# A Mamba layer between two feed-forward layers: the out projection as products of rounded halves

## Chip, cores and metric

One core of a Trainium2 chip. The metric is the device time of one execution in microseconds. Before the change three runs gave 1508.79, 1508.95 and 1509.53 us (median 1508.95).

## What is computed

The input is one sequence of 2048 tokens with 256 channels, float32. Three residual steps follow each other, each behind a layer norm: a gated feed-forward layer whose weights are looked up in a table of 16 values, a Mamba-2 layer of 64 heads of 64 channels with a state of 128, and the feed-forward layer again.

```python
x = x + 0.5 * ffn(layernorm(x))
x = x + mamba2(layernorm(x))
x = x + 0.5 * ffn(layernorm(x))
```

What matters of the Mamba layer (the reference works in chunks of 32 tokens, the kernel in chunks of 128, which gives the same sums):

```python
gate, hbc, dt = split(h @ in_proj_w)
hbc = silu(causal_conv4(hbc) + conv_b)              # x, B, C
dt = softplus(dt + dt_bias); cum = cumsum(-exp(A_log) * dt)
Y_diag = (C B^T * exp(cum_i - cum_j) * dt) @ x      # within a chunk
Y_off = exp(cum) * (C @ prev_states)                # from the chunks before
hidden = (Y_diag + Y_off + D * x) * silu(gate)
hidden = hidden * rsqrt(mean(hidden ** 2) + EPS) * norm_w
out = hidden @ out_proj_w
```

## The kernel before

The program is written out instruction by instruction: each engine (TensorE, VectorE, ScalarE, GpSimd, and SP, which issues the loads and stores) has a block with its own sequence, and semaphores order the engines among each other. An engine carries out its sequence strictly in the order in which it is written, so an instruction that waits holds up everything behind it.

First the weights of the feed-forward layer are decoded and that layer runs (24 ticks); the small projections for B, C and dt are made in its last ticks. Then comes the loop over the Mamba layer, from about 345 to 1368 us, and a second block with the second feed-forward layer.

The loop has 128 slots. The 64 heads are 32 pairs, taken in 8 groups of 4 pairs (GP = 4); a group goes through the 4 tiles of 512 tokens (TT), and in each tile through its 4 pairs. Slot v is thus pair v % 4 of its group and tile v // 4 % 4; 16 slots make a group. The loop is software-pipelined. In its step s (loops in lines 637, 903, 1009, 1311, 1616):

- TensorE (PE): states(s+2), turn_x(s+3) (a transpose), diag(s+1), the gate and x projections proj_g and proj_x of s+8, out_proj(s), off(s+2). The two projections are made of rounded halves (float32r): split_matmul gives hi x hi, hi x lo and lo x hi. The out projection is two exact fp32 products, on wo and hid.
- VectorE (DVE): the three conv taps of s+7 between the scans of s+2 (which carry the state from chunk to chunk), times_dt(s+3), skip_path(s+1) (writes hid), masked(s+2), scale_off(s+2), and after every fourth slot add_out(s), which takes the sum of four pairs out of PSUM.
- ScalarE (ACT): square(s), relus and exps of s+3 (the decays), evac_g and evac_x of s+8. With s % 4 = 0, here called the silu slot, the silus of four pairs come together between two loads of the activation table.
- GpSimd (POOL): add_squares(s), to_chunk_end(s+3) (makes xend, which the states need), in the silu slot the halo sums for the conv (not for tile 0), and gate(s+1), which multiplies hid by silu of the gate.
- SP: loads of cum_row(s+5), which waits for relus, and behind it e_row(s+4), and the weights of the next group.

The weights of the next group are prepared within a group by slot number u = s % 16: ScalarE makes the high halves (split_g_hi in u 6 and 8, split_x_hi in u 6 to 9) and scales the out weights (scale_wo in u 13 to 15 and in u 0 of the next group); GpSimd makes the low halves. They come at the end of the step of their engine.

## Time and profile before

| | |
|---|---|
| median of three runs | 1508.95 us |
| profiled execution, its time | 1511.01 us |
| profiled execution, its span | 1509.2 us |
| instructions in the span | 26250 |
| mean granted TensorE clock | 0.967 of full speed |

The profile is of one execution. Its page gives the busy time of each engine, and groups of instructions by line; the timeline gives instructions in order of time, with "idle before" in square brackets and the instruction that ended the idle time behind the arrow. "x4" counts instructions that were merged to one row; an exact fp32 product shows as two. The end of a matmul is modelled, so differences of starts say more than the lengths in the rows. PE is TensorE, PEld its weight loads.

### The profile page before, as it was taken

The page shows a single profiled execution, that of the slowest core. Times are in us where ns is not written, and L with a number is a line of the kernel's source. Part 1 is how long each engine was busy: PE and PEld are TensorE (multiplying, and loading weights), DVE is VectorE, ACT ScalarE, POOL GpSimd, SP SyncE. Part 2 cuts the span into 40 slices and gives each one's busy share as a digit, 9 for nine tenths or more (in the row PEclk, how much of TensorE's full clock was granted, in tenths as well). Part 3 has the DMA queues.
Part 4 walks back from the last instruction along what each step waited for, and adds up shares of the span by engine and source line. Part 5 has one row for each costly group of instructions (what it writes and reads, how often), then busy time and mean ns, then how long its engine had stood idle before and what let it go on. Part 6 is the DMA issues. An engine that isn't in the chain of part 4 may idle for free. (4 is left out here: it accounts for less than half of the span.)

```text
span 1509.2 us, 26250 instructions
## 1 busy us (share of the span) xinstructions
PE 1388.3 (92%) x8704; PEld 1091.1 (72%) x8704; DVE 1128.3 (75%) x2547; ACT 1040.4 (69%) x2133; POOL 680.6 (45%) x637
## 2 busy tenths in 40 slices
PE   4889977768999999999999999999999999986998
PEld 4878766556777777777777777777777777764787
DVE  5752444666988888897888889788888979896433
ACT  0124333576988888898888889888888988871332
POOL 1013211023656666566666656666665665661000
PEclk9999989889999999999999999999999999996999
DMA  5220000224344444343453533445444434334000
GB/s 125 71 88 25 15 15 14 69 43 102 106 105 113 123 104 114 99 107 105 110 127 100 112 98 113 103 113 122 108 108 93 116 103 112 101 95 181 15 14 28
DMA packets 102079, 136.36 MB, mean 90 GB/s; under 512 B 27744, under 2 KB 49856, under 8 KB 101824
## 3 DMA queue, kind: packets, MB, share of 16 engines
q1 hardware_dynamic: 99840, 132.67, 33.8%
q10 hardware_dynamic: 2112, 2.10, 0.4%
q8 instruction: 68, 1.11, 0.3%
q14 instruction: 59, 0.48, 0.1%
HBM read 124.76 MB, written 9.96 MB: 89 GB/s over the span
## 5 line engine op out<-in xcount | busy, mean ns | idle before, releaser
L843 ACT ACTIVATE M<-cum_row,cum_table 128x128 f32<-128x128 f32 x1024 | 311.8, 389 | 0.0
L1204 DVE SCALAR_TENSOR_TENSOR xs<-psum,conv_w_sb,xs 128x509 f32<-128x509 f32 (+2 forms) x384 | 284.9, 742 | 0.4
L994 POOL TENSOR_TENSOR xend<-xdt,to_end_table 128x512 f32<-128x512 f32 x128 | 148.9, 1164 | 298.1 <-DVE xdt L1215 298.1
L1592 PE MATMUL psum<-hid,wo 128*128 128x512 f32 x512 | 242.8, 596 | 9.1 <-ACT eT L754 8.8
L1000 POOL TENSOR_TENSOR hid<-hid,sg 128x512 f32<-128x512 f32 x128 | 241.8, 1889 | 0.1
L986 POOL TENSOR_TENSOR squares<-squares,sq 128x512 f32<-128x512 f32 x124 | 158.7, 1280 | 118.9 <-ACT sq L820 118.3
L1252 DVE TENSOR_TENSOR psum<-psum,e_row 128x512 f32<-128x512 f32 x128 | 89.5, 699 | 122.3 <-PE psum L1566 117.9
L1225 DVE TENSOR_TENSOR M<-M,CB 128x1024 f32<-128x1024 f32 x128 | 177.7, 1388 | 0.0
L1592 PEld LDWEIGHTS psum<-hid,wo 128*128 128x128 f32 x512 | 96.2, 189 | 84.1 <-issue 72.3
L1552 PE MATMUL psum<-xend,B_tok 128*128 128x128 f32 x1024 | 139.0, 279 | 17.5 <-POOL xend L994 17.2
L1577 PE MATMUL psum<-M,xdt 128*64 128x128 f32 x2048 | 142.7, 282 | 1.0 <-DVE psum L1252 0.9
L1552 PEld LDWEIGHTS psum<-xend,B_tok 128*128 128x128 f32 x1024 | 126.2, 194 | 22.7 <-POOL xend L994 21.7
L857 ACT ACTIVATE xs<-psum,conv_b_sb,conv_w_sb 128x512 f32<-128x512 f32 x128 | 98.6, 770 | 52.8 <-PE psum L40 47.2
L851 ACT ACTIVATE M<-M 128x1024 f32<-128x1024 f32 x128 | 134.4, 1050 | 0.5
L1577 PEld LDWEIGHTS psum<-M,xdt 128*64 128x64 f32 x2048 | 111.4, 138 | 22.9 <-issue 22.9
L825 ACT ACTIVATE sg<-psum 128x512 f32<-128x512 f32 x128 | 74.8, 585 | 75.7 <-PE psum L40 67.5
L1245 DVE SCALAR_TENSOR_TENSOR inner<-inner,decay_table,psum 128x64 f32<-128x64 f32 x512 | 118.3, 273 | 0.0
L38 PE MATMUL psum<-xT_hi,gw_hi 128*128 128x512 f32 x256 | 115.3, 450 | 2.2 <-DVE x_res L1062 1.5
L946 POOL TENSOR_TENSOR ffn_hidden_lo<-ffn_hidden,ffn_hidden_hi 128x512 fp32r<-128x512 f32 x24 | 30.8, 1284 | 182.6 <-ACT ffn_hidden_hi L669 182.6
L820 ACT ACTIVATE sq<-hid 128x512 f32<-128x512 f32 x124 | 77.6, 626 | 48.4 <-POOL hid L1000 48.2
L1566 PE MATMUL psum<-CT,inner 128*128 128x128 f32 x768 | 106.7, 275 | 0.0
L40 PE MATMUL psum<-xT_hi,gw_lo 128*128 128x512 f32 x256 | 102.2, 399 | 0.0
(200 smaller groups left out, 3024.3 us busy)
## 6 DMA issues: line engine op xcount, KB each, us to landing
cum_row<-cum_scratch SPq DMA_DIRECT2D x256, 256.0 KB, 4.4
e_row<-e_scratch SPq DMA_DIRECT2D x256, 128.0 KB, 3.5
xw_raw<-L_attn_in_proj_w_dram SPq DMA_DIRECT2D x32, 128.0 KB, 3.0
wo_raw<-L_attn_out_proj_w_dram SPq DMA_DIRECT2D x32, 128.0 KB, 3.1
gw_raw<-L_attn_in_proj_w_dram SPq DMA_DIRECT2D x16, 256.0 KB, 6.5
x_res<-_attn_hidden_states_dram ACTq DMA_DIRECT2D x4, 512.0 KB, 9.9
x_scratch<-x_res SPq DMA_DIRECT2D x4, 512.0 KB, 2.6
x_res<-x_scratch SPq DMA_DIRECT2D x1, 2048.0 KB, 8.7
```

The costliest lines, as they stand in the source:

```text
L38: nc.tensor.matmul(out, l_hi, r_hi, start=start, stop=False, skip_group_check=skip)
L843: last = nc.scalar.activation(M[:, v % 3, h, c * CH:(c + 1) * CH], cum_row[:, v % 2, h, c * CH:(c + 1) * CH], ACT.Relu, bias=scalar_of(CUM ...
L851: nc.scalar.activation(M[:, v % 3], M[:, v % 3], ACT.Exp, scale=-1.0).then_inc(exp_done, 1)
L986: nc.gpsimd.tensor_tensor(squares[:, tile(t)], squares[:, tile(t)], sq[:], ALU.add).then_inc(squares_done, 1)
L994: nc.gpsimd.tensor_tensor(xend[:, v % 2], xdt[:, v % 3], per_chunk_head(TO_END, v), ALU.mult).then_inc(xend_done, 1)
L1000: nc.gpsimd.tensor_tensor(hid[:, v % 2, :], hid[:, v % 2, :], sg[:, v % 8, :], ALU.mult).then_inc(hid_done, 1)
L1204: nc.vector.scalar_tensor_tensor(xs[:, v % 8, shift:], psum[:, X_BANK + v % 2, 0:TT - shift], tap_of(v, step), xs[:, v % 8, shift:], ALU.m ...
L1225: nc.vector.tensor_tensor(M[:, v % 3], M[:, v % 3], cb, ALU.mult).then_inc(M_done, 1)
L1245: nc.vector.scalar_tensor_tensor(after, before, scalar_of(CHUNK_DECAY, v, chunk, h), psum[:, ST_BANK, c * P + h * HP:c * P + (h + 1) * HP] ...
L1552: last = nc.tensor.matmul(psum[:, ST_BANK, c * P:(c + 1) * P], B_tok[:, t * CPT + c, :], xend[:, v % 2, c].rearrange("p h q -> p (h q)"), ...
L1577: last = nc.tensor.matmul(psum[h * HP:(h + 1) * HP, Y_BANK, c * CH:(c + 1) * CH], xdt[:, v % 3, c, h, :], M[:, v % 3, h, c * CH:(c + 1) * CH],
L1592: last = nc.tensor.matmul(psum[:, OUT_BANK + m, :], wo[:, j, m * P:(m + 1) * P], hid[:, v % 2, :], start=(j == 0), stop=(j == GP - 1))
```

## The change

The out projection is made of rounded halves, as the other projections are: six products (three for each half of the 256 output channels) instead of two.

- VectorE copies hid to hid_hi (hid_to_hi, rounded, two buffers) after the first scan of the step. GpSimd subtracts to make hid_lo (one buffer) at the start of its step. out_proj waits for both; skip_path waits for hid_lo_done instead of out_done.
- The weights: ScalarE scales wo_raw in place and copies to wo_hi; GpSimd makes wo_lo (split_wo_lo). The last of a group moves from u 0 to u 1.
- ScalarE's square(s+1) moves into the silu slot, between relus and exps.
- To make room, gw_raw is halved (each half of the gate weights is loaded when the one before is split; the splits move from u 6 and 8 to u 6 and 9), e_row and xend have one buffer instead of two and xdt two instead of three. e_row is loaded one slot later.
- The zero state is left out: in tile 0 the first chunk has no off product, its scan is a copy, and the scaling leaves its columns out.
- In the front the splits and scalings are put on ticks 4 to 7, 12 and 15.

The core of the diff:

```diff
-    gw_raw = sb("gw_raw", [P, KT, GP * P], F32)
+    gw_raw = sb("gw_raw", [P, KT, GP * P // 2], F32)
...
-    wo = sb("wo", [P, GP, D], F32)
...
+    wo_hi = sb("wo_hi", [P, GP, D], F32R)
+    wo_lo = sb("wo_lo", [P, GP, D], F32R)
...
-    e_row = sb("e_row", [P, 2, TT], F32)
-    xdt = sb("xdt", [P, 3, CPT, 2, HP], F32)
-    xend = sb("xend", [P, 2, CPT, 2, HP], F32)
+    e_row = sb("e_row", [P, TT], F32)
+    xdt = sb("xdt", [P, 2, CPT, 2, HP], F32)
+    xend = sb("xend", [P, CPT, 2, HP], F32)
     inner = sb("inner", [P, 2, CPT - 1, 2, HP], F32)
     carry = sb("carry", [P, 2, GP, 2, HP], F32)
+    hid_hi = sb("hid_hi", [P, 2, TT], F32R)
     hid = sb("hid", [P, 2, TT], F32)
+    hid_lo = sb("hid_lo", [P, TT], F32R)
...
+    G_TICKS = (4, 7)
+    WO_TICKS = (5, 6, 12, 15)
...
             def load_g_weights(q):
 
                 half = GP * P // 2
-                if q >= 2:
-                    sp.wait_ge(gw_lo_done, q - 1)
-                else:
-                    sp.wait_ge(w_small_lo, 2)
-                at = q % 2 * half
-                sp.dma_start(gw_raw[:, :, at:at + half], w_in_t[:, :, q * half:(q + 1) * half]).then_inc(gw_in[q % 2], 16)
+                if q >= 1:
+                    sp.wait_ge(gw_lo_done, q)
+                sp.dma_start(gw_raw[:], w_in_t[:, :, q * half:(q + 1) * half]).then_inc(gw_in, 16)
 
             def load_wo(p):
                 if p >= 2:
-                    sp.wait_ge(wo_done, p - 1)
+                    sp.wait_ge(wo_lo_done, p - 1)
...
-                sp.wait_ge(off_scaled, nth(v - 2))
+                sp.wait_ge(off_scaled, nth(v - 1))
...
-                if alive(s + 4):
-                    load_e(s + 4)
+                if alive(s + 3):
+                    load_e(s + 3)
                 g, u = divmod(s, SLOTS)
                 if s < 0 or g == GROUPS - 1:
                     continue
@@ -646,13 +650,14 @@
                     load_x_weights((g + 1) * GP + u - 2)
                 if u == 4:
                     load_g_weights(2 * (g + 1))
+                if u == 7:
...
             def scale_wo(p):
                 act.wait_ge(wo_in[p % 2], (p // 2 + 1) * 16)
                 if p < GP:
                     act.wait_ge(chan_in, 80)
-                else:
+                    act.wait_ge(w_small_lo, 2)
+                nc.scalar.activation(wo_raw[:, p % 2, :], wo_raw[:, p % 2, :], ACT.Copy,
+                                     scale=norm_sb[:, p:p + 1]).then_inc(wo_done, 1)
+                if p >= GP:
                     act.wait_ge(out_done, nth(last_of(p - GP)))
-                nc.scalar.activation(wo[:, p % GP, :], wo_raw[:, p % 2, :], ACT.Copy,
-                                     scale=norm_sb[:, p:p + 1]).then_inc(wo_done, 1)
+                act.wait_ge(wo_done, p + 1)
+                nc.scalar.activation(wo_hi[:, p % GP, :], wo_raw[:, p % 2, :], ACT.Copy).then_inc(wo_hi_done, 1)
...
-                if alive(s):
+                if alive(s) and (s < 0 or s % GP != 1):
...
+                if s >= 0 and s % GP == 0:
+                    square(s + 1)
...
-                if g < GROUPS - 1 and u in (6, 8):
-                    split_g_hi(2 * (g + 1) + u // 2 - 3)
+                if g < GROUPS - 1 and u in (6, 9):
+                    split_g_hi(2 * (g + 1) + u // 3 - 2)
                 if g < GROUPS - 1 and 6 <= u < 6 + GP:
                     split_x_hi((g + 1) * GP + u - 6)
                 if g < GROUPS - 1 and u >= 13:
                     scale_wo((g + 1) * GP + u - 13)
-                if g > 0 and u == 0:
+                if g > 0 and u == 1:
...
+            def split_wo_lo(p):
+                pool.wait_ge(wo_hi_done, p + 1)
+                if p >= GP:
+                    pool.wait_ge(out_done, nth(last_of(p - GP)))
+                nc.gpsimd.tensor_tensor(wo_lo[:, p % GP, :], wo_raw[:, p % 2, :], wo_hi[:, p % GP, :].bitcast(F32),
+                                        ALU.subtract).then_inc(wo_lo_done, 1)
+
+            def hid_to_lo(v):
+                pool.wait_ge(hid_hi_done, nth(v))
+                pool.wait_ge(out_done, nth(v - 1))
+                nc.gpsimd.tensor_tensor(hid_lo[:], hid[:, v % 2, :], hid_hi[:, v % 2, :].bitcast(F32),
+                                        ALU.subtract).then_inc(hid_lo_done, 1)
...
+                    hid_to_lo(s)
...
+                if g > 0 and u == 1:
+                    split_wo_lo(g * GP + GP - 1)
                 if s < 0 or g == GROUPS - 1:
                     continue
-                if u in (6, 8):
-                    split_g_lo(2 * (g + 1) + u // 2 - 3)
+                if u in (6, 9):
+                    split_g_lo(2 * (g + 1) + u // 3 - 2)
                 if 6 <= u < 6 + GP:
                     split_x_lo((g + 1) * GP + u - 6)
+                if u >= 13:
+                    split_wo_lo((g + 1) * GP + u - 13)
...
+            def hid_to_hi(v):
+                dve.wait_ge(hid_done, nth(v))
+                dve.wait_ge(out_done, nth(v - 2))
+                nc.vector.tensor_copy(hid_hi[:, v % 2, :], hid[:, v % 2, :]).then_inc(hid_hi_done, 1)
...
+                if chunk == 0:
+                    nc.vector.tensor_copy(inner[:, v % 2, 0].rearrange("p h q -> p (h q)"),
+                                          psum[:, ST_BANK, 0:P]).then_inc(scan_step, 1)
+                    return
...
-                nc.vector.tensor_tensor(bank(Y_BANK), bank(Y_BANK), e_row[:, v % 2, :], ALU.mult).then_inc(off_scaled, 1)
+                dve.wait_ge(e_in, (v + 1) * 32)
+                cols = slice(CH if at_slot(v)[1] == 0 else 0, TT)
+                nc.vector.tensor_tensor(psum[:, Y_BANK, cols], psum[:, Y_BANK, cols], e_row[:, cols],
+                                        ALU.mult).then_inc(off_scaled, 1)
 
             def skip_path(v):
                 j, t = at_slot(v)
                 dve.wait_ge(diag_done, nth(v))
-                dve.wait_ge(out_done, nth(v - 2))
...
+                if alive(s):
+                    hid_to_hi(s)
...
-                for c in range(CPT):
-                    if c > 0:
-                        before = inner[:, v % 2, c - 1]
-                    else:
-                        before = zero_state[:] if t == 0 else carry[:, t % 2, j]
+                first = 1 if t == 0 else 0
+                for c in range(first, CPT):
...
-                pe.wait_ge(hid_done, nth(v))
-                pe.wait_ge(wo_done, pair_of(v) + 1)
+                pe.wait_ge(hid_hi_done, nth(v))
+                pe.wait_ge(hid_lo_done, nth(v))
+                pe.wait_ge(wo_lo_done, pair_of(v) + 1)
...
-                    last = nc.tensor.matmul(psum[:, OUT_BANK + m, :], wo[:, j, m * P:(m + 1) * P], hid[:, v % 2, :],
-                                            start=(j == 0), stop=(j == GP - 1))
+                    cols = slice(m * P, (m + 1) * P)
+                    last = split_matmul(nc, psum[:, OUT_BANK + m, :], wo_hi[:, j, cols], wo_lo[:, j, cols],
+                                        hid_hi[:, v % 2, :], hid_lo[:], start=(j == 0), stop=(j == GP - 1))
```

## Rows read from the trace of the kernel before

**Rows 1.** The page: busy time of each engine over the span.

```profile
PE 1388.3 (92%) x8704; PEld 1091.1 (72%) x8704; DVE 1128.3 (75%) x2547; ACT 1040.4 (69%) x2133; POOL 680.6 (45%) x637
```

**Rows 2.** Timeline, TensorE, one plain slot: start us, length us, engine, line, operation.

```profile
763.41 0.40 PE L38 MATMUL psum<-xT_hi,xw_hi 128*128 128x512 f32 x1
...
764.81 1.88 PE L1592 MATMUL psum<-hid,wo 128*128 128x512 f32 x4
...
766.52 0.38 PE L1566 MATMUL psum<-CT,carry 128*128 128x128 f32 x2
...
767.41 1.06 PE L1552 MATMUL psum<-xend,B_tok 128*128 128x128 f32 x8
```

**Rows 3.** Timeline, VectorE, a plain slot from one scaling on.

```profile
791.65 0.70 DVE L1252 TENSOR_TENSOR psum<-psum,e_row 128x512 f32<-128x512 f32 x1 [1.20 <-PE psum L1566]
...
797.15 1.25 DVE L1225 TENSOR_TENSOR M<-M,CB 128x1024 f32<-128x1024 f32 x1
```

**Rows 4.** Groups by line and shape, before 345 us: total us, mean ns.

```profile
L1121 DVE TENSOR_TENSOR zmax<-zmax,ez 128x512 f32<-128x512 f32 x2 | 1.4, 691 | 0.1
...
L1118 DVE TENSOR_SCALAR ez<-ez 128x512 f32<-128x512 f32 x2 | 0.8, 414 | 0.0
...
L946 POOL TENSOR_TENSOR ffn_hidden_lo<-ffn_hidden,ffn_hidden_hi 128x512 fp32r<-128x512 f32 x24 | 30.8, 1284 | 182.6 <-ACT ffn_hidden_hi L669 182.6
```

**Rows 5.** Timeline, VectorE, adding out, then the silu slot.

```profile
768.22 1.28 DVE L1273 TENSOR_TENSOR mixed<-psum,mixed 128x512 f32<-128x512 f32 x2
...
774.37 1.25 DVE L1225 TENSOR_TENSOR M<-M,CB 128x1024 f32<-128x1024 f32 x1
...
777.00 0.22 DVE L1200 SCALAR_TENSOR_TENSOR xs<-psum,conv_w_sb,halo_sum 128x3 f32<-128x3 f32 x1 [0.54 <-POOL halo_sum L977]
```

**Rows 6.** Timeline, ScalarE, the same silu slot and the next.

```profile
777.35 1.28 ACT L851 ACT_TABLE_LOAD   x1
...
782.95 0.76 ACT L857 ACTIVATE xs<-psum,conv_b_sb,conv_w_sb 128x512 f32<-128x512 f32 x1
```

**Rows 7.** Timeline, GpSimd, a plain slot: the gate beside the masked product.

```profile
797.31 2.23 POOL L1000 TENSOR_TENSOR hid<-hid,sg 128x512 f32<-128x512 f32 x1
```

**Rows 8.** Timeline, TensorE: the output projections of four slots that follow each other.

```profile
796.79 1.88 PE L1592 MATMUL psum<-hid,wo 128*128 128x512 f32 x4
...
804.74 1.88 PE L1592 MATMUL psum<-hid,wo 128*128 128x512 f32 x4
...
812.83 1.88 PE L1592 MATMUL psum<-hid,wo 128*128 128x512 f32 x4
...
822.91 1.88 PE L1592 MATMUL psum<-hid,wo 128*128 128x512 f32 x4
```

**Rows 9.** Timeline, GpSimd and then TensorE, about slots 8 and 9.

```profile
812.24 1.29 POOL L958 TENSOR_TENSOR gw_lo<-gw_raw,gw_hi 128x512 fp32r<-128x512 f32 x1 [3.56 <-ACT gw_hi L693]
...
818.62 0.73 POOL L952 TENSOR_TENSOR xw_lo<-xw_raw,xw_hi 128x256 fp32r<-128x256 f32 x1
...
817.48 1.16 PE L1552 MATMUL psum<-xend,B_tok 128*128 128x128 f32 x8 [1.88 <-POOL xend L994]
```

**Rows 10.** Timeline, TensorE: diagonal products in slot 10 of two groups.

```profile
686.78 1.98 PE L1577 MATMUL psum<-M,xdt 128*64 128x128 f32 x16
...
819.00 1.09 PE L1577 MATMUL psum<-M,xdt 128*64 128x128 f32 x16
```

**Rows 11.** Timeline, GpSimd, two gates among the last slots.

```profile
1344.77 2.25 POOL L1000 TENSOR_TENSOR hid<-hid,sg 128x512 f32<-128x512 f32 x1
...
1350.00 2.26 POOL L1000 TENSOR_TENSOR hid<-hid,sg 128x512 f32<-128x512 f32 x1
```

**Rows 12.** Timeline, TensorE, states of slot 2 of a group.

```profile
882.19 1.16 PE L1552 MATMUL psum<-xend,B_tok 128*128 128x128 f32 x8 [0.36 <-POOL xend L994]
```

**Rows 13.** Groups by line in 340 to 1400 us: scans from the zero state.

```profile
L1245 DVE SCALAR_TENSOR_TENSOR inner<-zero_state,decay_table,psum 128x64 f32<-128x64 f32 x58 | 13.4, 274 | 0.0
```

**Rows 14.** The page: DMA issues; KB of each, us from issue to landing.

```profile
e_row<-e_scratch SPq DMA_DIRECT2D x256, 128.0 KB, 3.5
```

78 lines of the change are left out of this document (40 added, 38 removed).

## Prediction

> **What bounds the kernel now.** I began with the page's busy times. TensorE is busy for 92% of the span, VectorE for 75%, ScalarE for 69% and GpSimd for 45% [rows 1]. In the loop that the change edits, which holds most of the span, an average of the whole span hides how close the engines are, so I read one slot (one pair of heads times one tile of 512 tokens) on the timeline, engine by engine.
>
> TensorE: the six products of the x projection begin at 763.41, the output projection at 764.81, the off-diagonal products at 766.52, and the states of the next slot at 767.41 [rows 2]. So six rounded (split) products take 1.40 us, the two exact fp32 products of the output projection take 1.71 (the row's 1.88 is a modelled end; I use starts), and four off products take 0.89. From one output projection to the next are 7.95 us (796.79 to 804.74) and TensorE has no gap in them [rows 8]. A plain slot is bound by TensorE.
>
> VectorE in a plain slot: it waits 1.20 us for the off products before scaling them, and nowhere else [rows 3]. So it has 6.75 us of work. But once in four slots it also adds out the projection (1.28 us, start to next start 1.20), after which it is late: in that next slot (the silu slot, first of four) TensorE has to wait for VectorE's skip path before its off products, and the slot after begins with a 0.54 us wait for the halo sums [rows 5]. Four slots take 31.98 us (764.81 to 796.79 [rows 2, 8]) against 4 x 7.945 = 31.78.
>
> GpSimd has one more limit. Its gate takes 1.28 us of its own (as the same form of operation does elsewhere [rows 4]) but 2.23 when it starts beside the 1.25 us masked product of VectorE [rows 3, 7]. These two exclude one another.
>
> The worst slot: from 812.83 to 822.91 are 10.08 us [rows 8]. GpSimd waited 3.56 us for gw_hi, which ScalarE makes only at the end of the silu slot, so xend came late and TensorE waited 1.88 [rows 9]. That is 2.1 us in each of seven groups of sixteen slots. In three of the seven TensorE's granted clock then fell to the lower level (1.2 GHz) for some 3 us: the diagonal products, 1.09 at the upper level, took 1.98 [rows 10], and with the other products of those 3 us the slot was 1.55 longer again (from the starts of its output projections).
>
> **The change, part by part.** Durations are of the profiled execution; I add the sum to the median.
>
> 1. *Output projection, TensorE.* Six rounded products for two exact ones: 1.71 becomes 1.40, less 0.31 us in a slot. If TensorE bound all 128 slots, 40 us would go. With the plain slot then at 7.95 - 0.33 = 7.62 (0.02 by the closer spacing of such products, an estimate from [rows 2]).
>
> 2. *High half, VectorE.* Not in the trace. The nearest rows: a one-source operation over 128x512 from SBUF to SBUF took 414 ns, a two-source one 691 [rows 4]. I take 0.41 (start to start about 0.35, as all VectorE operations here follow some 0.07 before the modelled end), since a copy has one source; 0.69 stays as the upper bound, and the lower is 0.35, as the copy is certainly not free. It stands after the first scan, so everything of VectorE's queue waits for it, and it waits for the gate of the same head pair.
>
> VectorE then needs 6.75 + 0.35 = 7.10 in a plain slot, plus about 0.15 between the masked product and the scaling, which was hidden in the wait: 7.3. That is below 7.62. In the silu slot it starts 2.02 behind TensorE (0.82 as in a plain slot and 1.20 for adding out). Skip path done 5.5 after its start means off products at 7.55 rather than 6.73: the silu slot takes 8.5. In the next slot VectorE is 0.8 behind and waits 0.55 for halo sums (masked product to halo sum is unchanged, 2.63 us from 774.37 to 777.00 [rows 5]): 7.8. Then two of 7.62. Sum 31.6 against 31.98: **-0.4 us for four slots**, and not -1.3.
>
> 3. *Low half, GpSimd.* 1.28 us by the same form [rows 4]. It waits for hid_hi, and behind it in GpSimd's queue stand the squares, xend and the next gate. In a plain slot it ends 3.0 us after VectorE's slot began, 1.3 before the output projection wants it, and xend still follows its own input. So it is hidden where GpSimd has no other work. Where GpSimd also splits weights, it is not: with a split of gate weights (1.3) and x weights (0.7 [rows 9]) behind the gate, xend lands on the masked product and delays it by 0.4 to 0.8.
>
> By the Trainium skill, "SBUF — State Buffer", section "SBUF: two separate sides", VectorE and GpSimd lock a shared pair of ports for a whole instruction, for two SBUF inputs or a two-port mode; the gate's 2.23 agrees. By "VectorE: DVE Perf Modes", section "The perf-mode tier table", an fp32 copy within SBUF runs at two elements a cycle, which fits 414 ns and would make the copy a holder of that lock as well.
>
> 4. *Square moved ahead in the silu slot.* ScalarE ends its relus, then waits for the gate of the next slot, squares, and only then loads the exp table (at 777.35 now, right behind the relus [rows 6]). That wait is about 0.6 us, and with the square (0.53) the exps and all behind them come 1.1 later: evac_x, started at 782.95 now, reaches VectorE's next slot 0.3 late, which still fits into slack. In exchange GpSimd gets the square about 2 us sooner. The 0.36 wait of TensorE for xend at the third slot of a group [rows 12] goes, with 0.2 of slower starts around it: -0.6 for a group.
>
> 5. *Gate-weight split from slot 8 to slot 9, one raw buffer.* In slot 8 the x split remains, and GpSimd still waits for ScalarE's end of the silu slot before it; behind it now stand the x split (0.7), the masked product (1.25), the low half (1.28), squares (1.3) and xend (1.05). I get xend 5.5 us after GpSimd's restart, where today 5.2 pass (812.24 to 817.48 [rows 9]); and the output projection itself now waits, because the low half comes after that same point. Output projection of slot 8 to the states of slot 10 was 12.7; I get about 13.9: **+1.2 in each of seven groups**. The stall of TensorE is then over 3 us, so I take the lower clock in all seven instead of three: 4 x 1.55 = **+6.2**.
>
> 6. *Zero state left out* (tile 0, four of sixteen slots): one of four off chunks, 0.22, and a pair of scans of 274 ns [rows 13] replaced by a copy of 0.2 to 0.3: about -0.35 for a pair of slots.
>
> 7. *e_row with one buffer.* The load waits for the same scaling as before, but is needed one slot sooner. It lands 3.5 us after issue [rows 14] and has over 6: hidden, by 1 us in the silu slot, where it is queued on SP behind cum_row. xdt and xend with one buffer fewer wait for products that are over by then: nothing. Norm scaling of wo becomes scale and copy, one pass more on ScalarE, and 0.7 on GpSimd (the shape of the x split [rows 9]), four times in a group; in slots 1 and 13 to 15 this costs 0.5, as a late xend pushing the masked product. In the front the same steps, +1 us at most.
>
> 8. *The end.* The last slots have no projections; GpSimd binds them already, a gate every 5.23 us [rows 11]. Low half in that chain: +1.1 for some five slots, and +1.5 before the last product: **+6**.
>
> **Sum.** A group: slots 0 to 3: -0.4 - 0.6 - 0.35 + 0.5 = -0.85. Slots 4 to 7: -0.4 + 0.2 (splits) = -0.2. Slots 8 to 11: -0.4 + 1.2 + 0.1 = +0.9. Slots 12 to 15: -0.4 - 0.4 (the last tile has a pair of scans fewer, so the copy fits) - 0.3 (tile 0) + 0.1 = -1.0. Together -1.15, for seven groups -8; the last group -1; clock +6; end +6; front +1. That is +4. The profiled execution's span was 1509.2 and its time 1511.0, the median of the runs 1508.95; so I forecast 1508.95 + 4 to 5, **1514**.
>
> **Rivals.** *The gain survives (faster).* If VectorE's lateness is absorbed, the silu slot and the next stay at 7.95 and the others get 7.62: 31.14 for four, -0.84 x 32 = -27; tile 0 adds -7, the end +5: 1480. For it: TensorE has no gap in plain slots. Against: VectorE's slot with adding out is already 8 us of work. *The copy runs at one element a cycle (slower):* 0.69 instead of 0.41 is 0.28 more in the three slots of four where VectorE decides: 0.75 x 32 = +24: 1538. It decides from a copy of about 0.45. For it only that the output is of the rounded type; against it the 414 ns row. *More collisions of masked product and GpSimd (slower):* GpSimd's four operations, the copy and the masked product exclude each other and fill 6.6 of 7.9 us; if each four slots lose 0.5 more, 1530. *The change does not do what it says:* six products with six weight loads could run slower than the projections' 1.40, but those have the same shapes; I give it nothing.
>
> **How the numbers follow.** Forecast case 0.50, of which I give 0.06 to faster by over 0.2%, 0.12 to within and 0.32 to slower, as its terms are each good to some tenths of a us in 16 slots. The gain survives 0.30 (0.27 faster, 0.03 same). Slow copy 0.10 and more collisions 0.10, both slower. So faster 0.33, same 0.15, slower 0.52; 0.2% (3 us) is about what a measurement of this kernel can tell from no change. The forecast case alone spans 1500 to 1528. The range reaches halfway into the surviving gain, to 1482, and to the slow copy, 1540.
>
> **What would show it.** Right: output projection 1.40 start to start; hid_hi at 0.41; plain slots 7.6, silu slots 8.5; a stall of over 3 us at the output projection of slot 9 in each group, with the lower clock behind it; last slots over 6 us. Wrong: silu slots at 8 or less, slot 9 no longer than 10 us, hid_hi near 0.7, or masked products mostly over 1.6. A loss in a wait for e_row or for gw_raw would be a mechanism that I count at nothing.

## The result, and the profile after

The changed kernel takes 1526.32 us (median of 4 runs, 1518.78 to 1526.84) against 1509.01 for the kernel before in the same session: ratio 1.0103, 95% interval 1.0076 to 1.0130. It is slower by 17 us where I had forecast 5. The profiled execution is the quickest of the four (span 1517.1, mean granted clock 0.969); the other three had spans of 1524.5 to 1525.1 at clocks of 0.961 to 0.964.

The first lines of the page of after, in the columns of [rows 1]:

```profile
PE 1346.9 (89%) x8896; PEld 1127.2 (74%) x8896; DVE 1168.8 (77%) x2643; ACT 1050.9 (69%) x2165; POOL 868.0 (57%) x796
```

TensorE is busy for less time, as the change wants, and the span is longer. GpSimd has gone from 45% to 57%.

TensorE, timeline of after (start, us, instruction, count, idle time before it and what ended it). First the slot with the stall, then the output projection and what follows it in the next; the last row is of slot 14, which step 7 below comes back to:

```profile
812.65 0.47 PE L38 MATMUL psum<-hid_hi,wo_hi 128*128 128x512 f32 x1 [3.58 <-issue]
...
813.48 0.63 PE L38 MATMUL psum<-hid_hi,wo_hi 128*128 128x512 f32 x1
...
814.76 0.63 PE L1605 MATMUL psum<-CT,carry 128*128 128x128 f32 x2
815.18 1.49 PE L1605 MATMUL psum<-CT,inner 128*128 128x128 f32 x6
816.47 1.19 PE L1593 MATMUL psum<-xend,B_tok 128*128 128x128 f32 x8
...
821.94 0.39 PE L38 MATMUL psum<-hid_hi,wo_hi 128*128 128x512 f32 x1
822.17 0.40 PE L39 MATMUL psum<-hid_lo,wo_hi 128*128 128x512 f32 x1
...
823.32 0.38 PE L1605 MATMUL psum<-CT,carry 128*128 128x128 f32 x2
...
856.56 1.16 PE L1593 MATMUL psum<-xend,B_tok 128*128 128x128 f32 x8 [1.01 <-POOL xend L1016]
```

The output projection takes 1.38 us (821.94 to 823.32), and from it to the next are 7.61 (the next starts at 829.55). From the same rows over the whole loop come the distances between output projections, which I compare in four parts of a group of sixteen slots (slot 0 is the silu slot of tile 0). One group of each kernel from the same part of the loop (slot 9 is 10.08 in four groups before and about 11.65 in three; after, it is 9.2 to 9.3 in five and 7.68 in two), slots 0 to 3, 4 to 7, 8 to 11, 12 to 15:

| | 0-3 | 4-7 | 8-11 | 12-15 |
|---|---|---|---|---|
| before | 8.15 8.57 7.95 7.95 | 8.15 7.95 7.94 7.95 | 8.09 **10.08** 7.95 7.95 | 7.95 8.26 7.95 7.95 |
| after | 7.94 8.00 7.91 7.66 | 8.48 8.25 7.63 7.61 | **12.17 9.29** 7.61 7.61 | 7.97 8.16 8.71 7.38 |
| difference | -1.1 | 0.0 | +2.6 | +0.1 |

In the last group the tail grew as well (its last eight: 7.30 6.77 7.34 6.66 6.64 6.64 5.38 4.28, 51.0 us, for 42.9 before). From the first output projection to the last, after takes 1033.25 and before 1020.33, so +12.9. What lies behind is equal (+0.5). In this one profile the part ahead of the loop is 5.5 shorter (first output projection at 340.02 for 345.57), and its granted clock is higher. The windows view of before and of after (us, busy time and count of each engine, granted clock):

```profile
140.00:220.00 80.00, 68.74 (x350) 57.77 (x349) 35.33 (x78) 32.10 (x48) 15.39 (x12) 0.91 0.02 9
```
```profile
140.00:220.00 80.00, 64.09 (x359) 54.25 (x358) 39.23 (x87) 36.01 (x55) 15.86 (x14) 1.00 0.04 14
```

It is clock and not work: the kernel of experiment 4 has the same front, and its granted clock in this stretch is 0.91 and its first output projection stands at 345.42. Every other profile of a variant had it at 343.0 to 346.0. By its size this would explain most of the 7.5 us by which the profiled execution is quicker than the other three, of which there is only the mean clock to go by.

How the stall arises. GpSimd, ScalarE and VectorE around the slot of 12.17 (800.48 to 812.65):

```profile
801.49 1.05 POOL L1016 TENSOR_TENSOR xend<-xdt,to_end_table 128x512 f32<-128x512 f32 x1
802.52 2.22 POOL L1022 TENSOR_TENSOR hid<-hid,sg 128x512 f32<-128x512 f32 x1
809.58 1.75 POOL L961 TENSOR_TENSOR xw_lo<-xw_raw,xw_hi 128x256 fp32r<-128x256 f32 x1 [4.83 <-ACT xw_hi L689]
811.29 1.26 POOL L999 TENSOR_TENSOR hid_lo<-hid,hid_hi 128x512 fp32r<-128x512 f32 x1
812.51 1.29 POOL L1008 TENSOR_TENSOR squares<-squares,sq 128x512 f32<-128x512 f32 x1
813.75 1.05 POOL L1016 TENSOR_TENSOR xend<-xdt,to_end_table 128x512 f32<-128x512 f32 x1
```
```profile
796.59 0.63 ACT L828 ACTIVATE sq<-hid 128x512 f32<-128x512 f32 x1 [1.50 <-POOL hid L1022]
797.25 1.28 ACT L837 ACT_TABLE_LOAD   x1
...
806.20 0.62 ACT L828 ACTIVATE sq<-hid 128x512 f32<-128x512 f32 x1
806.84 1.28 ACT L859 ACT_TABLE_LOAD   x1
808.13 1.06 ACT L859 ACTIVATE M<-M 128x1024 f32<-128x1024 f32 x1
809.10 0.40 ACT L689 ACTIVATE xw_hi<-xw_raw 128x256 fp32r<-128x256 f32 x1
```
```profile
805.47 0.42 DVE L1240 CAST hid_hi<-hid 128x512 fp32r<-128x512 f32 x1
...
809.52 1.22 DVE L1259 TENSOR_TENSOR M<-M,CB 128x1024 f32<-128x1024 f32 x1
816.71 0.70 DVE L1291 TENSOR_TENSOR psum<-psum,e_row 128x512 f32<-128x512 f32 x1 [5.96 <-PE psum L1605]
```

hid_hi is ready at 805.89, but GpSimd stands at xw_lo until ScalarE ends the silu slot. The low half is queued behind it, and TensorE's output projection waits for that (the trace names only "issue"). VectorE then waits 5.96 us for TensorE. The x split itself takes 1.75 instead of 0.7, as it meets the masked product (VectorE's product M x CB) of 809.52.

Two smaller items stand in the waits of after for the stretch 500 to 1300 us (in total, times, longest):

```profile
POOL wo_lo L993 <- ACT wo_hi L710: 24.8, 17, 2.3
...
DVE psum L1291 <- DMA e_row<-e_scratch: 14.4, 17, 1.9
```

### The profile page after: what moved, and what is told of

Same layout as the page of the kernel before. It is cut to its first block and busy times, and to the rows that moved or that the text cites. A ratio compares the mean times of both kernels' runs of the same rounds, so it can differ in the third digit from the quotient of the medians.

```text
span 1517.1 us, 27235 instructions
## 1 busy us (share of the span) xinstructions
PE 1346.9 (89%) x8896; PEld 1127.2 (74%) x8896; DVE 1168.8 (77%) x2643; ACT 1050.9 (69%) x2165; POOL 868.0 (57%) x796
## 5 line engine op out<-in xcount | busy, mean ns | idle before, releaser
L999 POOL TENSOR_TENSOR hid_lo<-hid,hid_hi 128x512 fp32r<-128x512 f32 x128 | 165.5, 1293 | 155.1 <-DVE hid_hi L1240 155.1
L1022 POOL TENSOR_TENSOR hid<-hid,sg 128x512 f32<-128x512 f32 x128 | 246.0, 1922 | 0.0
L1016 POOL TENSOR_TENSOR xend<-xdt,to_end_table 128x512 f32<-128x512 f32 x128 | 144.8, 1131 | 51.0 <-DVE xdt L1249 39.9
L1008 POOL TENSOR_TENSOR squares<-squares,sq 128x512 f32<-128x512 f32 x124 | 161.9, 1306 | 0.0
L1291 DVE TENSOR_TENSOR psum<-psum,e_row 128x512 f32<-128x512 f32 (+1 forms) x128 | 85.0, 664 | 91.9 <-PE psum L1605 69.8
L38 PE MATMUL psum<-hid_hi,wo_hi 128*128 128x512 f32 x256 | 104.5, 408 | 45.6 <-issue 35.9
L1616 PEld LDWEIGHTS psum<-M,xdt 128*64 128x64 f32 x2048 | 109.9, 136 | 31.6 <-issue 31.5
L1605 PE MATMUL psum<-CT,inner 128*128 128x128 f32 x768 | 110.9, 282 | 4.3 <-DVE hid L1300 3.9
L1605 PEld LDWEIGHTS psum<-CT,inner 128*128 128x128 f32 x768 | 100.2, 197 | 12.2 <-DVE carry L1283 5.1
L833 ACT ACTIVATE sg<-psum 128x512 f32<-128x512 f32 x128 | 74.5, 582 | 41.6 <-PE psum L40 33.4
```

Of the source, the lines that this page charges most:

```text
L38: nc.tensor.matmul(out, l_hi, r_hi, start=start, stop=False, skip_group_check=skip)
L999: nc.gpsimd.tensor_tensor(hid_lo[:], hid[:, v % 2, :], hid_hi[:, v % 2, :].bitcast(F32), ALU.subtract).then_inc(hid_lo_done, 1)
L1008: nc.gpsimd.tensor_tensor(squares[:, tile(t)], squares[:, tile(t)], sq[:], ALU.add).then_inc(squares_done, 1)
L1016: nc.gpsimd.tensor_tensor(xend[:], xdt[:, v % 2], per_chunk_head(TO_END, v), ALU.mult).then_inc(xend_done, 1)
L1022: nc.gpsimd.tensor_tensor(hid[:, v % 2, :], hid[:, v % 2, :], sg[:, v % 8, :], ALU.mult).then_inc(hid_done, 1)
L1605: last = nc.tensor.matmul(psum[:, Y_BANK, c * CH:(c + 1) * CH], before.rearrange("p h q -> p (h q)"), CT[:, tok:tok + CH], start=(c == fir ...
```

## The experiments

All ratios are to the kernel before, run beside the variant. "Groups" are sums of sixteen distances as in the table: 130.8 or 132.3 before, 130.4 to 133.6 after (132.2 on average); before, the first group is 131.5.

**1. The x splits taken away from slot 8.** The changed kernel, and the kernel before, with:

```diff
+    X_SLOTS = (5, 6, 7, 9)
...
-                if u in (7, 8):
-                    load_x_weights((g + 1) * GP + u - 5)
+                if u in (6, 7):
+                    load_x_weights((g + 1) * GP + u - 4)
...
-                if g < GROUPS - 1 and 6 <= u < 6 + GP:
-                    split_x_hi((g + 1) * GP + u - 6)
+                if g < GROUPS - 1 and u in X_SLOTS:
+                    split_x_hi((g + 1) * GP + X_SLOTS.index(u))
```

(the same for split_x_lo; in the kernel before the gate splits also go to 6 and 9).

> The changed kernel with nothing split in the silu slot 8 of a group: the x splits move from slots 6 to 9 to slots 5, 6, 7 and 9, their loads with them. Theory (GpSimd waits for ScalarE's end of the silu slot before an x split, and the low half behind it starves the output projection): the step from slot 8 to 9 falls from 12.17 to about 8.5 us and the next from 9.2 to about 7.9, 5 us in each of seven groups, 35 in all: 1526 becomes about 1490, below the kernel before. Rival (the shared ports are so full that the stall only moves to another slot): at most 10 us are won, 1516.

> The kernel before with the same move of the x splits, and the second gate split in slot 9 as in the change. Theory: its own stall of 2.1 us in seven groups and the 1.55 of lower clock behind it in three go, 19 us: 1490. Then the change itself, compared with equal placement, is worth about nothing (within 5 us). Rival (the change makes its own stall, the one of before has another cause): 1505 to 1509 here.

Changed kernel: 1508.33, ratio 0.9982 (0.9971 to 0.9994). Kernel before: 1494.08, ratio 0.9892 (0.9874 to 0.9909). The stall itself is proved: the slot of 12.17 became 8.45, and 18 us of the change's time went with it. In the kernel before, 8.09 and 10.08 or 11.65 became 8.07 and 8.60, which gave 16. But the changed kernel did not come near 1490. Its next slot took 9.55, because two things were late there, e_row and the gate split. VectorE and TensorE of off8:

```profile
808.84 0.70 DVE L1292 TENSOR_TENSOR psum<-psum,e_row 128x512 f32<-128x512 f32 x1 [1.81 <-DMA e_row<-e_scratch]
...
810.55 1.48 DVE L1241 CAST hid_hi<-hid 128x512 fp32r<-128x512 f32 x1
```
```profile
809.69 1.09 PE L1617 MATMUL psum<-M,xdt 128*64 128x128 f32 x16 [0.77 <-DVE psum L1292]
811.81 0.50 PE L38 MATMUL psum<-xT_hi,gw_hi 128*128 128x512 f32 x1 [1.02 <-POOL gw_lo L968]
```

e_row waits had been 14.4 us in 17 cases; here they were 28.7 in 25, the longest of 4.3 us in the last group, whose slot 1 took 13.31 for 9.31. Part of what the stall had covered came out behind it.

The pair also says where the change still loses when both kernels have their splits in the same slots: 14 us, where I had expected at most 5. The two loops differ by 13.2 us in the profiles, and 12.5 of it is in the last group (112.0 for 99.5: the e_row wait and the longer tail). The first seven groups are level (129.7 and 129.6 on average), although the changed kernel leaves out the zero state there, which experiment 8 prices at 0.9 a group.

**2. The low half left out.** GpSimd's subtraction of hid_hi is dropped. TensorE's three products stay (it reads hid_hi where it read hid_lo, an edit not shown), and so does GpSimd's wait for hid_hi. The output lacks the low half's share.

```diff
-                nc.gpsimd.tensor_tensor(hid_lo[:], hid[:, v % 2, :], hid_hi[:, v % 2, :].bitcast(F32),
-                                        ALU.subtract).then_inc(hid_lo_done, 1)
+                pool.sem_inc(hid_lo_done, 1)
```

> The changed kernel without the low half of hid: GpSimd's subtraction is left out, and TensorE reads the high half a third time in its place, so that TensorE's and VectorE's work is the same and the output lacks the low half. Theory (the low half is hidden in plain slots and costs where GpSimd has other work): plain slots stay 7.6 and silu slots 8.5; slot 8 to 9 falls by 1.2, the slots with wo splits lose 1 to 2 us for a group, the end 6 to 8: about 1503. Rival A (the low half is hidden everywhere): 1524 to 1526. Rival B (the ports shared by GpSimd and VectorE bind all slots): silu slots fall to 8.1 too, 1490 or less.

1490.85, ratio 0.9874 (0.9853 to 0.9895): the low half costs 35 us, half as much again as I expected. Where: GpSimd waits for xw_hi nearly as long as before (27.1 us in six groups, 28.9 in after), but TensorE's output projection doesn't stand behind that:

```profile
801.86 0.47 PE L38 MATMUL psum<-hid_hi,wo_hi 128*128 128x512 f32 x1 [0.32 <-issue]
...
805.75 1.16 PE L1592 MATMUL psum<-xend,B_tok 128*128 128x128 f32 x8 [1.41 <-POOL xend L1015]
```

Slot 8 took 8.90 for 12.17, the slot behind 9.34, the lower clock was gone, and slot 14 took 7.5 for 8.7. Groups were 128.3 for 132.2 on average, so 28 us in seven: 19 of them in slots 8 to 11, 8 in slots 12 to 15. The last eight distances were 44.6 for 51.0, so 6 more (and 3 back in this profile, by one slot of 12.33 in the last group, where VectorE waits 3.4 us for e_row). The silu slot did not move (8.49), nor did the plain ones (7.60): there the low half is hidden, as step 3 had it.

**3. The high half copied twice.**

```diff
+                nc.vector.tensor_copy(hid_hi[:, v % 2, :], hid[:, v % 2, :]).then_inc(copy_step, 1)
+                dve.wait_ge(copy_step, nth(v))
                 nc.vector.tensor_copy(hid_hi[:, v % 2, :], hid[:, v % 2, :]).then_inc(hid_hi_done, 1)
```

> The changed kernel with the copy of the high half on VectorE made twice (0.35 us more in each slot). Theory (VectorE decides the silu slot and the one after, TensorE the two plain ones): silu slot 8.48 to 8.83, the next by 0.35, plain ones by 0 to 0.1: about +0.8 for four slots, +24: 1550. Rival A (TensorE bound): 1526 to 1530. Rival B (VectorE bound in all slots): +45, 1571.

1544.16, ratio 1.0219 (1.0200 to 1.0239). 18 us for 128 copies of 0.42 (54 us): most of them are hidden. The silu slot went only to 8.69, plain slots to 7.7 to 8.0, and slot 8 became shorter (10.72), while the one ahead of it took 8.62 for 7.61: the same lateness, met one slot sooner. The second copy adds 0.45 us to VectorE's queue (from the first copy to the next operation 0.79 for 0.34, as it waits for the first). As that lengthens a plain slot by 0.1 to 0.4, VectorE has at most 0.35 us left in a plain slot of the change.

**4. e_row loaded ahead of cum_row** in SyncE's step.

```diff
+                if alive(s + 3):
+                    load_e(s + 3)
                 if alive(s + 5):
                     load_cum(s + 5)
-                if alive(s + 3):
-                    load_e(s + 3)
```

> The changed kernel with the load of e_row put ahead of the load of cum_row in each step of SP. Theory (with one buffer e_row lands too late in the slots behind a silu slot, because its load is queued behind cum_row's wait for the relus; the trace of the changed kernel shows 17 waits for it, 14.4 us in 800 of the loop): these waits go, 10 to 15 us of the time: about 1513. Rival (the waits lie beside other waits): within 3 us of the changed kernel, 1523 to 1526.

1527.02, ratio 1.0097 (1.0078 to 1.0115). The e_row waits went, the slot behind the silu slot fell from 8.25 to 7.87, and nothing was won in all. In this profile the slot behind the stall took 10.2 to 10.3 in six of seven groups, and 9.29 or 7.68 in that of the change: more of the lower clock (below). Slot 5 gave back 3.8 us over the eight groups, and slot 9 took 9.2 more. So e_row's single buffer is a real wait, and removing it alone does not shorten the change as it stands. Whether it would with the stall gone was not tried by itself: experiment 7 has both edits, and no wait for e_row between 500 and 1300 us.

**5. The square back at the start of the step.**

```diff
-                if alive(s) and (s < 0 or s % GP != 1):
+                if alive(s):
                     square(s)
...
-                if s >= 0 and s % GP == 0:
-                    square(s + 1)
```

> The changed kernel with the square at the start of every step again, as before the change. Theory (the square ahead costs ScalarE a wait of 0.6 us but lets GpSimd go on 2 us earlier in the slot after the silu slot, and GpSimd has no slack of 2 us there): slower by 5 to 15 us, 1531 to 1541. Rival (the wait of ScalarE is what matters): faster, 1515 to 1520.

1518.44, ratio 1.0040 (1.0024 to 1.0057): quicker than the change, where I expected slower. Slot 8 fell from 12.17 to 11.62, about ScalarE's 0.6 for the square in the silu slot (GpSimd's restart is 8.58 us behind the output projection of slot 8 and was 9.10), and slots 13 to 15 from 24.25 to 23.69; slot 1 is longer in most groups (9.15 for 8.00).

**6. A placement of all splits by the free slots, with e_row first** (gate splits at 5 and 7, x splits at 6, 6, 7, 9, output weights at 14, 14, 15, 2), on the changed kernel, and the same placement on the kernel before.

```diff
+    X_SLOTS = (6, 6, 7, 9)
+    G_SLOTS = (5, 7)
+    WO_SLOTS = (14, 14, 15)
...
-                if u == 7:
+                if u == 6:
                     load_g_weights(2 * (g + 1) + 1)
```

> The changed kernel with e_row's load first, and no weight split in a silu slot or the slot after it, save one x split in slot 9: gate splits in slots 5 and 7, x splits in 6, 6, 7 and 9, out weights in 14, 14, 15 and 2. Theory: every four slots take 8.5 + 7.8 + 7.6 + 7.6 = 31.5 us, so the 128 slots 28 us less than in the changed kernel's 132.3 for sixteen (126 for sixteen in seven groups is 44 less): 1480 to 1484. Rival (VectorE and GpSimd exclude each other so often that splits cost wherever they stand): 1495 to 1500.

> The kernel before with the same placement of the splits (its e_row has two buffers, its loads stay in order). Theory (its losses are at slots 1, 9 and 13, from ScalarE being late after the silu slot): 31.98 for each four slots, 127.9 for sixteen, where 129.25 were measured with the x splits moved alone: 1484 to 1487. The changed kernel with this placement is then faster by 3 us or so, the rounded products' gain less the silu slots' loss and the longer end.

1583.33, ratio 1.0468 (1.0451 to 1.0486), and 1576.56, ratio 1.0449 (1.0405 to 1.0493). They missed by 100 and 90 us, for a reason that is not the question: the loads stand too late in SyncE's queue for such splits. ScalarE in the first:

```profile
554.31 0.42 ACT L694 ACTIVATE xw_hi<-xw_raw 128x256 fp32r<-128x256 f32 x1 [5.81 <-DMA xw_raw<-L_attn_in_proj_w_dram]
```

The third x load stands in SyncE's slot 7 there, and its split in ScalarE's slot 7. In the stretch 500 to 1300 us ScalarE waits 39.5 us in 6 cases for x weights and 40.0 in 5 for output weights; in the other kernel of the pair 33.4 in 8 and 29.2 in 5. In all the other kernels a load stands at least one slot ahead of its split. The pair tells only that it must.

**7. The same idea with early loads**: x splits at 5, 6, 9, 10, gate splits at 5 and 7, their loads first in SyncE's slot, e_row ahead of cum_row, the square back; and the splits alone on the kernel before.

```diff
+    X_SLOTS = (5, 6, 9, 10)
+    G_SLOTS = (5, 7)
...
+                if s >= 0 and g < GROUPS - 1 and u == 6:
+                    load_g_weights(2 * (g + 1) + 1)
+                if s >= 0 and g < GROUPS - 1 and u in (6, 7):
+                    load_x_weights((g + 1) * GP + u - 4)
+                if alive(s + 3):
+                    load_e(s + 3)
```

**8. Only the edits that make room**: exact output projection with one wo as before, no halves, all else as in the change but for the square.

```diff
-                    last = split_matmul(nc, psum[:, OUT_BANK + m, :], wo_hi[:, j, cols], wo_lo[:, j, cols],
-                                        hid_hi[:, v % 2, :], hid_lo[:], start=(j == 0), stop=(j == GP - 1))
+                    last = nc.tensor.matmul(psum[:, OUT_BANK + m, :], wo[:, j, m * P:(m + 1) * P], hid[:, v % 2, :],
+                                            start=(j == 0), stop=(j == GP - 1))
```

> The changed kernel with the four x splits at slots 5, 6, 9 and 10 of a group, the two gate splits at 5 and 7, the loads that feed them put first in SyncE's slot and one slot earlier, e_row loaded ahead of cum_row, and the square back at its old place. So no split stands behind the silu slot's long ScalarE work, no load is late for its split, and e_row is a place further ahead. Theory (the cost of the change is in its collisions with the splits in the middle of a group, and the plain slots keep their gain): slot 8 to 9 about 8.2, 9 to 10 about 8.7, no granted clock lost there, 1488 (1480 to 1496). Rival (VectorE, ScalarE and GpSimd are together full enough that the late work only moves): the wait comes back in slots 5 to 7 or 10 to 11, and the time stays at 1503 or more.

> The kernel before with its x splits at slots 5, 6, 9 and 10 and its gate splits at 5 and 7; its loads stay, since it has two raw buffers of each. Theory (the wait for gw_hi behind the silu slot is all that was wrong there; with both weight splits away from slot 8 nothing is late): 1490 (1486 to 1494), slots 8 to 10 near 8.0 each. Compared with the place2b kernel this tells whether the rounded output projection gives anything once the splits stand well: by the theory of the collisions the two lie within 5 us of each other, since the silu slots (8.5 for 8.1) eat most of the 0.33 a plain slot. Rival: the loads come late for the splits at slot 5 (ScalarE waits for a DMA), 1500 or more.

> The edits that make room, without what the room is for: gate weights raw in one buffer with their split at slots 6 and 9, one buffer for e_row and xend, two for xdt, no zero state, the last output weights one slot later, the square back at its old place; the output projection stays exact fp32 with its two products, and neither the high nor the low half is made. The buffers keep their places in memory. Theory (the loss of the change is the low half and the copy in VectorE's and GpSimd's queues, and the edits that make room give about as much as they take): the left-out zero state gives 7 us, the gate split at slot 9 and the e_row load with one buffer take some of it back, so 1500 to 1508. Plain slots 7.95 as before, slot 8 to 9 about 8.6 (no gate split queued there), slot 9 to 10 about 10. Rival (the single buffers and the later split are what costs): 1515 or more, with waits of VectorE for e_row in most silu slots.

place2b 1505.07, ratio 0.9961 (0.9945 to 0.9977); before_place2 1496.88, ratio 0.9905 (0.9879 to 0.9930); room 1491.17, ratio 0.9868 (0.9841 to 0.9895).

place2b, the kernel of experiment 7, lies where its rival had it (1503 or more). Slots 8 and 9 came down to 8.42 and 8.63 with no clock lost, and slot 6 went up to 8.22 and slot 1 to 9.5 to 11.4 in all groups but the first, in two of them with lower clock. Slot 13 took 8.93, but that is the square and not the placement: it is 8.92 in experiment 5. TensorE's wait for xend, 4.9 us in 5 cases in after, had moved there:

```profile
PE psum L1595 <- POOL xend L1018: 19.7, 18, 2.1
```

before_place2 lies above its own bounds, as ScalarE waited for a gate load in some groups (8.8 us in 6 cases). The two are 8 us apart where I had expected at most 5, and once more it is the last group: 108.6 for 99.5, while the first seven groups are both 129.5 on average.

The room kernel is the most telling one. Its groups are 128.6 to 129.4. The zero state gives 0.9 a group, as 7.95, 7.95 and 8.15 in slots 14, 15 and 0 become 7.72 each. e_row waits are there as in after (14.7 us, 18 times). The gate split at slot 9, which I had booked as a loss, is a gain: 10.08 or 11.65 became 8.90 with no lower clock. GpSimd and TensorE of room:

```profile
801.99 0.74 POOL L956 TENSOR_TENSOR xw_lo<-xw_raw,xw_hi 128x256 fp32r<-128x256 f32 x1 [3.35 <-ACT xw_hi L688]
802.69 1.27 POOL L990 TENSOR_TENSOR squares<-squares,sq 128x512 f32<-128x512 f32 x1
803.92 2.03 POOL L998 TENSOR_TENSOR xend<-xdt,to_end_table 128x512 f32<-128x512 f32 x1
```
```profile
806.01 1.16 PE L1561 MATMUL psum<-xend,B_tok 128*128 128x128 f32 x8 [0.45 <-POOL xend L998]
```

GpSimd still waits 3.35 for ScalarE, yet with no gate split behind that wait TensorE loses 0.45 where it had lost 1.88 [rows 9].

**9. Room, with the x splits of experiment 1.**

> The kernel that only makes room (exact output projection, no halves), with the x splits at slots 5, 6, 7 and 9 and their loads a slot earlier, as in the off8 kernels. In the room kernel GpSimd still waits 3.4 us for the x split behind the silu slot (xw_lo for xw_hi, 20.1 us in 6 groups) and slot 9 to 10 takes 8.90. Theory: the two gains are of the same slots, so little adds: 9 to 10 becomes 8.6 as in the before_off8 kernel (its other slots had 129.25 a group, less 0.9 for the zero state gives 128.3, where the room kernel has 128.6 to 129), 1488 (1485 to 1491). Rival (the gains add, as the stall had cost the kernel before 15 us by itself): 1480 or less.

1490.61, ratio 0.9864 (0.9839 to 0.9889): slot 9 fell to 8.59 and the time stayed. The two cures treat the same slot. In this profile slot 9's 2 us are lost again in one slot of the last group (12.23 for 8.91), where VectorE waits 3.9 us for e_row. Against off8, which has the same room and the same slots for its splits, this kernel is 18 us quicker: that is about the price of the rounding with the stall of slot 8 gone (the square stands differently in the two). Both room kernels are quicker than the kernel before and the changed one.

## Why the prediction was right and wrong

The sign was right, and so was the mechanism of slot 8: GpSimd's queue behind the silu slot holds back the output projection. The size was not: the sum had +4 to 5 and the runs +17, inside the range. Set beside the distances of the profiles (us, seven groups and the last), the sum shows where it missed:

| | forecast | measured |
|---|---|---|
| slots 0 to 3 | -6 | -6.6 |
| slots 4 to 7 | -1.4 | +1.0 |
| slots 8 to 11, with the clock | +12.5 | +10.3 |
| slots 12 to 15 | -7 | +0.1 |
| last group and end | +5 | +8.1 |
| loop | +3 | +12.9 |

So the largest miss is not the stall but slots 12 to 15, 7 of the 10 us, and the end is 3. The sum had +1 for the front, which in this one profile is -5.5. The +0.5 behind the loop and some 4 us that the loops of the two profiles do not show are the rest of the 17.

The ratios of the runs give this account: before 1509, the edits that make room -20 (0.9868), three products with copy and weight splits but no low half next to nothing more (0.9874), the low half +35. (The square stands differently in the second and third, which experiment 5 prices at 8 us in the change; in these two it was not tried alone.)

- **Step 1, the output projection:** right. 1.38 for the 1.40 forecast, plain slots 7.61 for 7.62.
- **Step 2, the copy:** right. 0.42 measured, silu slot 8.48 for 8.5, next 8.25 for 7.8 (e_row adds some: 7.87 in experiment 4), then 7.63 and 7.61: 32.0 for 31.6. The slow-copy rival fell with it. In the profiles, the sum of all that the rounding does without the low half is near nothing: 0.6 less in a group (128.3 for 128.9 in room), against 4 us more in the last group, 3.4 of them in the one slot of 12.33.
- **Step 3, low half hidden in plain slots:** right (experiment 2). In slots with splits it cost more than the 0.4 to 0.8: 8 us over seven groups in slots 12 to 15, 1.2 a group.
- **Step 4, square ahead:** the gain of slots 0 to 3 came (-1.1 for -0.85), but "fits in slack" was wrong. Where the x split follows the silu slot, ScalarE's 0.6 goes straight into the stall, and the whole edit costs time.
- **Step 5, the stall:** it came, and the size of slots 8 to 11 came out (35.08 without lower clock, for 34.96 by the sum), but partly by luck, as the chain was wrong in two places. I had GpSimd's chain from its restart to xend at 5.5 us; it took 5.2 (809.58 to the end of xend at 814.80). What I took as fixed was the moment of the restart. It lies 9.10 us behind the output projection of slot 8 (800.48 to 809.58), and was 7.50 before (804.74 to 812.24 [rows 8, 9]). 1.3 of the 1.6 lie ahead of the silu slot: in the slot before, ScalarE's square waits 1.50 us for GpSimd's gate (0.54 before), and its first table load is 3.23 ahead of the output projection of slot 8 (797.25 to 800.48), where it was 4.53 ahead (800.21 to 804.74). The square in the silu slot adds 0.6, and the split that GpSimd waits for is shorter (0.40 for the gate split's 0.62), which makes the other 0.3. ScalarE in the kernel before:

```profile
799.56 0.63 ACT L820 ACTIVATE sq<-hid 128x512 f32<-128x512 f32 x1 [0.54 <-POOL hid L1000]
800.21 1.28 ACT L829 ACT_TABLE_LOAD   x1
```

  So GpSimd waits for ScalarE, which had waited for GpSimd. The kernel without the low half (experiment 2) tells how much of the delay is the low half's. Its output projection of slot 8 starts at 792.95; ScalarE, then GpSimd:

```profile
788.77 0.63 ACT L828 ACTIVATE sq<-hid 128x512 f32<-128x512 f32 x1 [1.21 <-POOL hid L1021]
789.42 1.28 ACT L837 ACT_TABLE_LOAD   x1
```
```profile
801.75 0.73 POOL L961 TENSOR_TENSOR xw_lo<-xw_raw,xw_hi 128x256 fp32r<-128x256 f32 x1 [4.53 <-ACT xw_hi L689]
```

  The table load is 3.53 ahead and the restart 8.80 behind. So without the low half 1.3 of the 1.6 are still there: the low half has 0.3, the square and the shorter split 0.3. The remaining 1.0 is VectorE's place: its xdt, which GpSimd's xend and gate follow, starts 8.24 ahead of that output projection in both kernels with the copy, and 9.23 ahead before. That VectorE runs later against TensorE because of the copy and of TensorE's shorter slots is argued from the rows, not tried.

  Without lower clock the two slots take 12.17 + 7.68 = 19.85 against 18.17: +1.7 where I had +1.2. The sum still came out, probably because it had added the lateness of the silu slot beside the stall, which covers it. What I compared with was wrong too: room has 16.98 in these two slots, so moving the gate split gives 1.2 a group and the clock. Against that, copy and square, less the shorter products, cost 1.3 (18.24 without the low half), and the low half itself 1.6 and the lower clock.
- **Clock:** I forecast the lower level in all seven groups for three before. In the profiled execution it came in five, in that of experiment 4 in all, and longer. Right in kind; my +6 is +3 here, and by the mean clocks of the other three runs more than that there.
- **Step 6, zero state:** right, 0.9 a group for the 0.65 that the sum had.
- **Step 7, "e_row: nothing; wo splits 0.5":** the step that failed by most. For slots 12 to 15 the sum had only 0.1 for the wo splits. Without the low half these four slots take 30.9, which is the -1.0 forecast and a little more; with it they take 32.2, so the low half beside the wo splits costs 1.2 there. e_row waits in 17 slots, and slot 14 takes 8.71 for 7.38 beside it, since xend lands on the masked product (2.11 for 1.05) behind a wo split that waited 1.97 for ScalarE. GpSimd there:

```profile
851.17 0.74 POOL L993 TENSOR_TENSOR wo_lo<-wo_raw,wo_hi 128x256 fp32r<-128x256 f32 x1 [1.97 <-ACT wo_hi L710]
...
854.40 2.11 POOL L1016 TENSOR_TENSOR xend<-xdt,to_end_table 128x512 f32<-128x512 f32 x1
```

- **Step 8, the end:** +8.1 for +6, a gate chain with one more operation, as worked out. GpSimd of after:

```profile
1367.62 1.27 POOL L999 TENSOR_TENSOR hid_lo<-hid,hid_hi 128x512 fp32r<-128x512 f32 x1 [0.54 <-DVE hid_hi L1240]
1368.85 1.28 POOL L1008 TENSOR_TENSOR squares<-squares,sq 128x512 f32<-128x512 f32 x1
1370.09 1.27 POOL L1022 TENSOR_TENSOR hid<-hid,sg 128x512 f32<-128x512 f32 x1
```

The rival "the gain survives" had 1480, which no kernel reached; the nearest, 1491, came from the edits that only make room.

Open: the clock of the unprofiled runs is known only as a mean, so the last 4 of the 17 us are not placed. With the splits well placed the change still loses in the last group, and no experiment treats that group by itself.

## What to carry to other kernels

An operation that is free in a plain stretch can be dear where its engine waits for another: it is then queued behind that wait, and everything that needs it inherits the wait. Ask not only what stands behind a wait but when the wait will end, as a chain through other engines (VectorE's xdt, GpSimd's gate, ScalarE's square, GpSimd's split) moves that moment too: 1.6 us here. Look at every place where two such operations meet, and not only at the worst: here the quiet slots 12 to 15 had the larger error. And try the edits that make room for a change by themselves: here they were worth 20 us, and the change that they were made for cost 35.

## What the runs showed of the hardware

*The copy and GpSimd exclude each other in both directions.* The cast to hid_hi takes 0.42 alone. In off8 it started at 810.55, as GpSimd was in the 1.27 us subtraction of 810.49, and took 1.48. GpSimd's next split, at 811.71 with the copy still running to 812.03, took 0.93 for 0.73:

```profile
811.71 0.93 POOL L962 TENSOR_TENSOR xw_lo<-xw_raw,xw_hi 128x256 fp32r<-128x256 f32 x1
```

In after 14 of the 97 between 500 and 1300 us took 0.65 to 0.75. By the Trainium skill, "SBUF — State Buffer", section "SBUF: two separate sides", the two engines lock a shared port pair for whole instructions; this case agrees, and the copy, one source and all, is a party to it.

*The same wait of TensorE ends in several ways.* After 3.6 us without a product the profiled execution of the change went on at the upper level of the clock (2.4 GHz) in two groups. In five the products fell to the lower level (1.2 GHz) within 1.3 us after work had begun again (in the group shown above after 0.8, at 813.48), which cost 1.5 to 1.6 us (9.2 to 9.3 for 7.68). In six groups of experiment 4 the first product was already at it:

```profile
819.95 0.77 PE L38 MATMUL psum<-hid_hi,wo_hi 128*128 128x512 f32 x1 [3.60 <-issue]
820.51 0.63 PE L39 MATMUL psum<-hid_lo,wo_hi 128*128 128x512 f32 x1
...
824.35 1.63 PE L1593 MATMUL psum<-xend,B_tok 128*128 128x128 f32 x8
```

and the slot took 10.3, 2.6 more. A product of that shape then starts 0.43 us after the one before instead of 0.23. The first product does not decide the price: in one group of the change (680.35) it was as slow, and the slot took 9.21, since the state products were back at 1.06 there (684.22), where experiment 4 has 1.63. In experiment 5, behind 3.0 us without a product, all of this occurs within seven groups: 7.7 twice, 9.1 and 9.3, and 10.4 to 10.5 three times. So a stall of this length costs between nothing and 2.8 us beyond itself, and which it is cannot be told from the stall.

*Shorter waits can do it too.* In the kernel before, after 1.88 us without a product the products fell to the lower level in three of seven groups [rows 9, 10]. In place2b, in slot 1, they did so after 1.42 and 1.74 us in two groups:

```profile
613.01 1.96 PE L1595 MATMUL psum<-xend,B_tok 128*128 128x128 f32 x8 [1.42 <-POOL xend L1018]
```

The granted clock was 1.00 from 608.9 to 612.0 and 0.70 from 612.0 to 615.0, and the slot took 11.12. In the next group 1.53 us in the same place (before 743.85) left the clock alone, and the slot took 9.63. Waits of 1.96 and 2.08 us in two other groups left it alone too (10.14 and 10.19).
